# Attention between two routed feed-forward layers: all shared tiles first, batch 1's norm chain later in the ring, stores, loads and bias adds moved

## The chip, the cores and the metric

One core of one Trainium2 chip runs the whole program in one launch. The metric is device time in microseconds (us), the median of several executions. The engines are TensorE (PE, with its weight loads as PEld), VectorE (DVE), ScalarE (ACT), GpSimd (POOL) and SyncE (SP), each with its own program in order; they meet at semaphores. SP, ACT and POOL also issue DMA transfers.

## The reference

The input is `(2, 1024, 128)` float32: two batches of 1024 tokens.

```python
x = x + 0.5 * ffn(layernorm(x))
x = x + attention(layernorm(x))          # 16 heads of 8, causal
x = x + 0.5 * ffn(layernorm(x))

def expert(h, g, u, d):                  # 128 -> 352 -> 128
    return einsum('...i,hi->...h', silu(h @ g.T) * (h @ u.T), d)
def ffn(x):                              # 1 shared expert, top 2 of 7 routed ones
    out = expert(x, sg, su, sd)
    for e in range(7):
        out = out + w[..., e:e+1] * expert(x, rg[e], ru[e], rd[e])
def attention(x):
    v = x @ w_v + v_b
    q = (x @ w_q + q_b) @ w_k.T + k_b    # the keys are x itself
    probs = softmax(causal(q . x / sqrt(8)))
    return (probs @ v) @ c_proj_w + c_proj_b
```

## The kernel before, in words

**First feed-forward layer.** Tokens stand in 16 tiles of 128. The list `JOBS[0]` sets the order of the work: 13 tiles for the shared expert (`BEFORE[0]`), then 38 tiles of routed rows (`NJ`), then the last 3 shared tiles; 54 jobs (`NQ`). At step s PE does the first matmuls of job s (`up_pe`, L899 to L901), the transposes of job s-1 (`act_tr_pe`, L919) and the last matmuls of job s-2 (`down_pe`, L933); ACT does silu (L1000) and a copy (L1008), DVE the product (L1043) and the eviction (L1079 routed, L1081 shared). Routed rows are first sorted by expert: POOL scatters 32 blocks of rows to DRAM (L1174), two halves of 16, and SP loads them back tile by tile (L1260). `batch_at` says ahead of which step PE transposes a batch of loaded tiles (L953); routed tiles 0 to 9 need the first half sorted, tiles 10 and up both. POOL scatters each routed result back to DRAM (L1197), and `results_load` (L1271) reads the results of 8 token tiles, batch 0 after routed tile 21, batch 1 after the last one, 37.

**Between the layers.** The tokens are four chunks of 512 (`NCH`), chunks 0 and 1 being batch 0. For each: weighting (L1126) and adding (L1138) the results, statistics (`n_stats`, L504), `rstd` on POOL (L519), `z` on ACT (L540), transposes (`n_tr`, L573), a high and a low part (`n_hi` L579, `n_lo` L585), queries (`q_pe`, `q_act`, low part L1571 or L1145) and values (`v_pe`, L1508 to L1510, `v_act` L1543, bias L1553). The tables `FRONT_PE`, `BEHIND_ACT` and so on give the step of the feed-forward loop at which batch 0's pieces run; batch 1's pieces on PE and DVE run in the ring, at the places of `SECOND_PE` and `SECOND_DVE`. Keys and queries are written to DRAM (L1578) and read back, one group of 4 heads at a time (L1928, L1936).

**Attention.** 8 groups of 4 heads, 4 to a batch. The row maxima of a group are found first: PE makes the scores (L1605, with a causal mask by L1608), DVE reduces them (L1757). These are "ring" items, at most 4 in flight. The prologue `RING_PROLOGUE` has 54: 38 maxima of group 0, the first of group 1, two transposes of the maxima (`mrow`, L1628), 13 more of group 1. DVE turns the maxima into a high and a low part (L1761 to L1765), copies them out (L1771), and SP writes them into the queries' spare rows (L1949); then the exponent units start: PE L1648, ACT L1816, and PE's products with the values L1677. From then on each group is a body in which PE goes through an order written out by hand (`ORDERS`): units of its group, the last 24 maxima of the next group and the first 14 of the group after that, four of these ahead of that body's `mrow` transposes.

**The queue of SP** in `attn_sp` is a list in order too, and each wait in it holds back all that stands behind. Keys of group 2 share memory with `q_f`, `q_h`, `q_l`, so `keys_clear` (L1421) waits until all queries are stored; the loads of group 2 wait until the clearing has landed.

## Time and profile before

| what | value |
|---|---|
| median of 3 runs | 570.33 us (570.11 to 571.1) |
| profiled execution, its own time | 571.84 us |
| span of its trace | 570.0 us |
| mean granted clock of PE | 0.972 |
| PE busy | 521.1 us, 91% |
| DVE, ACT, POOL busy | 388.5, 319.8, 272.1 us |

Busy shares are means over stages with different limits: first the layer with its sorting (to about 163 us), then the crossing into attention (to about 200 us), attention in bodies of 29.5 us, and the second layer. What a change in one stage is worth has to be read in that stage.

### The profile page before, as it was taken

The page shows a single profiled execution, that of the slowest core. Times are in us where ns is not written, and L with a number is a line of the kernel's source. Part 1 is how long each engine was busy: PE and PEld are TensorE (multiplying, and loading weights), DVE is VectorE, ACT ScalarE, POOL GpSimd, SP SyncE. Part 2 cuts the span into 40 slices and gives each one's busy share as a digit, 9 for nine tenths or more (in the row PEclk, how much of TensorE's full clock was granted, in tenths as well). Part 3 has the DMA queues.
Part 4 walks back from the last instruction along what each step waited for, and adds up shares of the span by engine and source line. Part 5 has one row for each costly group of instructions (what it writes and reads, how often), then busy time and mean ns, then how long its engine had stood idle before and what let it go on. Part 6 is the DMA issues. An engine that isn't in the chain of part 4 may idle for free.

```text
span 570.0 us, 11374 instructions
## 1 busy us (share of the span) xinstructions
PE 521.1 (91%) x3574; PEld 406.0 (71%) x3574; DVE 388.5 (68%) x1013; ACT 319.8 (56%) x678; POOL 272.1 (48%) x417
## 2 busy tenths in 40 slices
PE   5985969999996799999999999999999889889995
PEld 2884969998954465656666666565746889889995
DVE  5694635557367888887979888888555775445744
ACT  4552424457444276776767677677776444434643
POOL 8299887667356711212120303030318888854540
PEclk9899789999996899999999999999999999999999
DMA  8922424132861581505050505020001031431414
GB/s 283 294 67 50 111 77 120 45 107 81 242 183 56 170 190 35 173 2 175 2 174 1 176 0 176 1 102 2 2 2 33 31 91 43 118 92 34 125 50 121
DMA packets 41384, 54.65 MB, mean 96 GB/s; under 512 B 6064, under 2 KB 32176, under 8 KB 40560
## 3 DMA queue, kind: packets, MB, share of 16 engines
q1 hardware_dynamic: 32528, 42.70, 26.4%
q0 software_dynamic: 4480, 9.25, 4.9%
q10 hardware_dynamic: 4320, 1.98, 1.3%
q8 instruction: 32, 0.52, 0.4%
q14 instruction: 24, 0.20, 0.1%
HBM read 34.03 MB, written 28.00 MB: 109 GB/s over the span
## 4 chain that ended last, share of the span: by engine, by line
PE 57%; issue 18%; POOL 10%; DMA 6%; DVE 4%; SPq 2%; ACT 2%; ACTq 1%; another core or an unknown queue 1%; POOLq 0%; DVEq 0%
PE psum L1605 11%; PE psum L1648 11%; PE psum L1677 10%; PE psum L933 6%; POOL z_rows L1174 6%; PE psum L919 3%; PE psum L901 3%; PE psum L899 3%; PE psum L900 3%; PE psum L1608 2%; POOL idle L1184 2%; DMA b_p<-in_attn_c_proj_b 2%; DMA yc<-y_rows 1%; DMA y_rows<-ys,to_row 1%; PE psum L1633 1%
## 5 line engine op out<-in xcount | busy, mean ns | idle before, releaser
L1757 DVE TENSOR_REDUCE mxp<-psum 128x1 f32<-128x512 f32 (+3 forms) x304 | 179.0, 654 | 32.9 <-PE psum L1605 32.1
L1816 ACT ACTIVATE probs<-psum 128x512 f32<-128x512 f32 (+1 forms) x304 | 154.9, 578 | 39.8 <-PE psum L1648 37.2
L1863 POOL TENSOR_SCALAR_AFFINE_SELECT probs<-probs 128x512 f32<-128x512 f32 x64 | 40.0, 635 | 174.2 <-ACT probs L1816 174.2
L1648 PE MATMUL psum<-queries,keys 128*128 128x512 f32 (+3 forms) x384 | 122.5, 381 | 0.6 <-DMA queries<-m_rows 0.3
L1605 PE MATMUL psum<-keys,queries 128*128 128x512 f32 (+1 forms) x304 | 116.1, 417 | 2.9 <-DVE mxp L1757 2.4
L1000 ACT ACTIVATE silu<-psum 128x352 f32<-128x352 f32 x107 | 49.6, 463 | 99.5 <-PE psum L901 62.6
L1197 POOL DMA_INDIRECT y_rows<-ys,to_row x76 | 74.3, 977 | 59.1 <-DVE ys L1079 35.4
L1043 DVE TENSOR_TENSOR act<-silu,psum 128x352 f32<-128x352 f32 x107 | 55.6, 519 | 68.0 <-ACT silu L1000 41.7
L933 PE MATMUL psum<-wall_f,at 128*128 (+1 forms) x648 | 92.2, 279 | 2.7 <-DVE x L1081 1.8
L1648 PEld LDWEIGHTS psum<-queries,keys 128*128 128x128 f32 x384 | 66.8, 191 | 26.8 <-ACT probs L1816 12.6
L933 PEld LDWEIGHTS psum<-wall_f,at 128*128 128x128 f32 x648 | 82.1, 194 | 4.1 <-ACT at L1008 2.3
L1605 PEld LDWEIGHTS psum<-keys,queries 128*128 128x128 f32 x304 | 58.1, 194 | 18.1 <-DVE mxp L1757 7.8
L1677 PE MATMUL psum<-probs,vg 128*32 128x512 f32 (+3 forms) x768 | 69.8, 491 | 0.4 <-POOL probs L1863 0.4
L919 PE MATMUL psum<-ident,act 128*128 128x128 f32 x324 | 54.7, 278 | 5.9 <-DVE act L1043 4.4
L899 PE MATMUL psum<-wall,zs_h 128*128 x152 | 56.9, 374 | 1.0 <-issue 1.0
L1008 ACT COPY at<-psum 128x384 f32<-128x384 f32 x108 | 51.3, 475 | 11.0 <-PE psum L919 9.7
L900 PE MATMUL psum<-wall,zs_h 128*128 x152 | 50.4, 331 | 0.0
L901 PE MATMUL psum<-wall,zs_l 128*128 x152 | 50.2, 330 | 0.0
L919 PEld LDWEIGHTS psum<-ident,act 128*128 128x128 f32 x324 | 41.0, 142 | 12.3 <-DVE act L1043 8.2
L1677 PEld LDWEIGHTS psum<-probs,vg 128*32 128x32 f32 x768 | 21.1, 109 | 35.4 <-issue 22.9
L1174 POOL DMA_INDIRECT z_rows<-zrow,slots x32 | 34.4, 1076 | 15.9 <-DVE slots L750 10.5
L1174 POOL DMA_INDIRECT z_rows<-zrow_late,slots x32 | 31.2, 975 | 5.8 <-issue 5.8
(240 smaller groups left out, 732.4 us busy)
## 6 DMA issues: line engine op xcount, KB each, us to landing
z_rows<-q_stack SPq DMA_DIRECT2D x12, 682.5 KB, 5.6
keys<-k_stack SPq DMA_DIRECT2D x32, 128.0 KB, 5.9
queries<-q_stack SPq DMA_DIRECT2D x8, 512.0 KB, 5.3
zg_early<-z_rows SPq DMA_DIRECT2D x44, 65.0 KB
yc<-y_rows SPq DMA_DIRECT2D x10, 256.0 KB, 4.0
zg_late<-z_rows SPq DMA_DIRECT2D x32, 65.0 KB
k_stack<-zt_h SPq DMA_DIRECT2D x8, 256.0 KB, 2.9
q_stack<-q_h SPq DMA_DIRECT2D x8, 256.0 KB, 3.7
```

Source lines behind the costliest of these rows:

```text
L899: e.matmul(dst, zh, weight(K.wall, base, hi, HID), start=True, stop=False)
L900: e.matmul(dst, zh, weight(K.wall, base, lo, HID), start=False, stop=False)
L901: ins = e.matmul(dst, zl, weight(K.wall, base, hi, HID), start=False, stop=True)
L919: ins = e.transpose(bank(K, at_bank(f, q))[:, k * P:(k + 1) * P], K.act[:, q % 2, k * P:(k + 1) * P], K.ident[:, :])
L933: ins = e.matmul(bank(K, Y_BANK)[:, 0:EMB], K.at[:, q % 2, k * P:(k + 1) * P], weight(K.wall_f, base, DN + k * EMB, EMB), start=(k == 0), ...
L1174: e.indirect_dma_start(K.z_dram[f], bass.IndirectOffsetOnAxis(ap=K.slots[:, g:g + 1], axis=0), K.zrow[f][:, t, :], None).then_inc(K.z_sc[t ...
L1197: e.indirect_dma_start(K.y_dram[f], bass.IndirectOffsetOnAxis(ap=K.to_row[:, j:j + 1], axis=0), K.ys[:, j % RING_Y, :], None).then_inc(K.y ...
L1605: ins = e.matmul(dst, K.queries[u][:, i * P:(i + 1) * P], K.keys[u][:, heads[0]:heads[-1] + 1, k0 * P:(k0 + nb) * P], start=True, stop=Tru ...
L1648: ins = e.matmul(slot(K, u, d, n)[:, m * (q1 - q0):(m + 1) * (q1 - q0)], K.keys[v][:, j, kt * P:(kt + 1) * P], K.queries[v][:, q0:q1], sta ...
L1677: ins = e.matmul(bank(K, O_BANK)[32 * j:32 * j + 32, q0 - half * CHUNK:q1 - half * CHUNK], K.vg[:, kt, j, :], probs_of(K, n)[:, j, :], sta ...
L1757: e.tensor_reduce(K.mxp[:, heads[0]:heads[-1] + 1, i, which], scores, AX.X, ALU.max).then_inc(K.A["taken"], 1)
L1816: e.activation(probs_of(K, product)[:, heads[0]:heads[-1] + 1, :], src, ACT.Exp, scale=SCALE).then_inc(K.A["ex"], 1)
```

## The change

Six edits, each an order of work:

1. `BEFORE[0]` is 16: all shared tiles stand ahead of the routed ones, and the batch with routed tile 10 is transposed one step later relative to the tiles.
2. The values of batch 0 (`v` 0 and 1) leave the loop's last steps and run in the ring, ahead of items 0 and 2; ACT evicts them behind the issue of batch 1's `results_load`. They use banks 6 and 4.
3. Batch 1's pieces stand 5 or 6 items later in the ring.
4. On SP, chunk 1's queries are stored for heads 0 to 3 first, group 0's queries are loaded on that, and the other 12 heads are stored behind.
5. The store of batch 1's keys moves from SP to ACT; the store of its queries moves on SP from ahead of `rows_load` (L1949) to behind it.
6. `proj_bias_pool` (L2060), four adds in a row on POOL at the crossing, becomes two ahead of `v_bias_pool(0)` and two inside attention, behind the bodies of groups 1 and 2.

```diff
-BEFORE = (13, 11)
+BEFORE = (TT, 11)
-ONE_AT_AGAIN = (43, NQ)
+ONE_AT_AGAIN = (46, NQ)
 def batch_at(f, step):
-        if step == BEFORE[f] + j - (min(b, 2) if f == 0 else 1 if j == WHOLE else 2):
+        if step == BEFORE[f] + j - min(2 if f else b, 1 if j == WHOLE else 2):
...
 def v_pe(K, c):
     if c == 0:
-        e.wait_ge(K.A["qf"], 1)
+        e.wait_ge(K.A["qf"], 2)
     elif c == 1:
-        e.wait_ge(K.A["qf"], 2)
+        e.wait_ge(K.FF[0]["yev"], NQ)
...
-SECOND_DVE = {13: (("n_stats", 2),), 16: (("n_stats", 3),), 20: (("n_lo", 2),), 26: (("n_lo", 3),)}
+SECOND_DVE = {18: (("n_stats", 2),), 21: (("n_stats", 3),), 26: (("n_lo", 2),), 32: (("n_lo", 3),)}
...
         elif r == 2:
-            e.wait_ge(K.A["vev"], 1)
+            e.wait_ge(K.A["qf"], 1)
...
 def attn_pool(K):
     e = K.nc.gpsimd
+    e.wait_ge(K.NS[1]["z"], NCH)
     e.wait_ge(K.A["vb"], NCH)
     for p in range(LOOP3):
         for u in range(3):
             pool_body(K, p, u, LOOP)
+            if (p, u) in ((0, 1), (0, 2)):
+                proj_bias_pool(K, u + 1)
...
 def attn_sp(K):
-    for c in range(NCH // 2):
-        keys_sp(K, c)
-        queries_sp(K, c)
+    keys_store(K, e, 0)
+    queries_sp(K, 0)
+    keys_store(K, e, 1)
+    queries_sp(K, 1, (0, 4))
     for c in range(NCH // 2):
         e.wait_ge(K.k_st[c], 16 * 3)
     e.wait_ge(K.wiped, 2 * WIPES)
     keys_load(K, 0, 0, 0)
-    for c in range(NCH // 2):
-        e.wait_ge(K.q_st[c], 16 * 3)
+    e.wait_ge(K.q_st[0], 16 * 3)
+    e.wait_ge(K.q_first, 16 * 3)
+    queries_load(K, 0, 0, 0)
+    queries_sp(K, 1, (4, HEADS))
     e.wait_ge(K.FF[0]["mix"], 4)
-    queries_load(K, 0, 0, 0)
     keys_load(K, 0, 0, 1)
+    e.wait_ge(K.q_st[1], 16 * 3)
     queries_load(K, 0, 0, 1)
-    for c in range(NCH // 2, NCH):
-        keys_sp(K, c)
+    rows_load(K, 0, 0, 0, RING_PROLOGUE.index(("mrow", 0, 0)))
     for c in range(NCH // 2, NCH):
         queries_sp(K, c)
-    rows_load(K, 0, 0, 0, RING_PROLOGUE.index(("mrow", 0, 0)))
     for c in range(NCH // 2, NCH):
         e.wait_ge(K.k_st[c], 16 * 3)
         e.wait_ge(K.q_st[c], 16 * 3)
     keys_clear(K, 2)
...
             results_load(K, e, 0, 1, (0, 1))
+            v_act(K, 0)
+            v_act(K, 1)
...
             q_act(K, 2)
+            keys_store(K, e, 2)
             q_act(K, 3)
+            keys_store(K, e, 3)
```

On PE, where the first layer ends and the ring begins, before (`wall_f,at` are the last matmuls of a job, `keys,queries` ring items 0 and 1, `ident_b,mask_b` their masks):

```order
L900 MATMUL psum<-wall,zt_h 128x352
L901 MATMUL psum<-wall,zt_l 128x352
L919 MATMUL psum<-ident,act 128x128 x3
L933 MATMUL psum<-wall_f,at 128x128 x3
L919 MATMUL psum<-ident,act 128x128 x3
L933 MATMUL psum<-wall_f,at 128x128 x6
L1605 MATMUL psum<-keys,queries 128x512
L1608 MATMUL psum<-ident_b,mask_b 128x512
```

The same place in the changed kernel (`wv,zt` are the value matmuls, 12 to a chunk; the last three of chunk 0, ring items 0 and 1, and the first three of chunk 1):

```order
L1509 MATMUL psum<-wv_h,zt_h 128x128
L1510 MATMUL psum<-wv_l,zt_h 128x128
L1511 MATMUL psum<-wv_h,zt_l 128x128
L1607 MATMUL psum<-keys,queries 128x512
L1610 MATMUL psum<-ident_b,mask_b 128x512
L1607 MATMUL psum<-keys,queries 128x512
L1610 MATMUL psum<-ident_b,mask_b 128x512
L1509 MATMUL psum<-wv_h,zt_h 128x128
L1510 MATMUL psum<-wv_l,zt_h 128x128
L1511 MATMUL psum<-wv_h,zt_l 128x128
```

The shared tile ahead of the ring is gone, and the value matmuls of batch 0 now stand around its first two items.

On SP, at the crossing, before (`queries<-m_rows` is `rows_load`, `keys<-q_stack` is `keys_clear`, the last two rows are the loads of group 2):

```order
L1578 DMA q_stack<-q_h 16x8x512 x2
L1578 DMA q_stack<-q_l 16x8x512
L1578 DMA q_stack<-q_h 16x8x512 x2
L1578 DMA q_stack<-q_l 16x8x512
L1949 DMA queries<-m_rows 4x8x128 x2
L1421 DMA keys<-q_stack 32x4096 x4
L1928 DMA queries<-q_stack 128x1024
L1936 DMA keys<-k_stack 32x1024 x4
```

On SP, the same place in the changed kernel, from the load of group 0's queries on:

```order
L1934 DMA queries<-q_stack 128x1024
L1579 DMA q_stack<-q_h 12x8x512 x2
L1579 DMA q_stack<-q_l 12x8x512
L1942 DMA keys<-k_stack 32x1024 x4
L1934 DMA queries<-q_stack 128x1024
L1955 DMA queries<-m_rows 4x8x128 x2
L1579 DMA q_stack<-q_h 16x8x512 x2
L1579 DMA q_stack<-q_l 16x8x512
L1579 DMA q_stack<-q_h 16x8x512 x2
L1579 DMA q_stack<-q_l 16x8x512
L1422 DMA keys<-q_stack 32x4096 x4
```

The six stores of batch 1's queries have moved from ahead of the maxima's transfer to between it and the clearing; the load of group 0's queries stands ahead of 12 heads' stores.

## Rows read from the trace of the kernel before

**Rows 1.** Windows: length, busy PE, PEld, DVE, ACT, POOL, granted clock, DMA share, GB/s.

```profile
163.70:193.60 29.90, 22.57 (x84) 13.73 (x83) 25.67 (x56) 14.22 (x33) 17.22 (x26) 0.83 0.42 126
196.40:199.80 3.40, 3.13 (x8) 1.50 (x8) 2.87 (x6) 0.00 (x0) 1.44 (x2) 0.53 0.34 77
205.00:234.50 29.50, 29.50 (x204) 18.68 (x203) 24.33 (x48) 20.65 (x41) 5.52 (x10) 1.00 0.49 130
```

**Rows 2.** PE in order of time: start, duration; in brackets idle before, releaser.

```profile
56.44 0.50 PE L953 MATMUL psum<-ident,zg_early 128*128 128x128 f32 x2 [4.90 <-DMA zg_early<-z_rows]
82.05 0.66 PE L953 MATMUL psum<-ident,zg_early 128*128 128x128 f32 x2 [4.67 <-DMA zg_early<-z_rows]
149.51 0.31 PE L1508 MATMUL psum<-wv_h,zt_h 128*128 128x128 f32 x1
150.88 0.38 PE L899 MATMUL psum<-wall,zs_h 128*128 x1
162.84 0.48 PE L1605 MATMUL psum<-keys,queries 128*128 128x512 f32 x1
```

**Rows 3.** The chain that ended last: start, duration, what.

```profile
76.18 2.39 DMA z_rows<-zrow,slots
96.69 0.67 PE psum L933 x6
98.67 0.67 PE psum L933 x6
...
158.96 4.07 DMA y_rows<-ys,to_row
163.70 3.52 DMA yc<-y_rows
```

**Rows 4.** DVE from the last routed tile to the maxima's parts.

```profile
158.39 0.29 DVE L1079 COPY ys<-psum 128x128 f32<-128x128 f32 x1
163.12 0.29 DVE L1081 SCALAR_TENSOR_TENSOR x<-psum,x 128x128 f32<-128x128 f32 x1 [1.09 <-PE psum L933]
163.70 7.33 DVE L1757 TENSOR_REDUCE mxp<-psum 128x4 f32<-128x512 f32 x13
179.41 0.69 DVE L1757 TENSOR_REDUCE mxp<-psum 128x1 f32<-128x512 f32 x1 [1.93 <-PE psum L1605]
193.90 1.19 DVE L1763 CAST mm_hl<-nmax 128x32 fp32r<-128x32 f32 x1
195.13 1.20 DVE L1765 TENSOR_TENSOR mm_hl<-nmax,mm_hl 128x32 fp32r<-128x32 f32 x1
223.06 0.52 DVE L1763 CAST mm_hl<-nmax 128x32 fp32r<-128x32 f32 x1
```

**Rows 5.** POOL beside the maxima's parts.

```profile
192.57 4.93 POOL L2060 TENSOR_TENSOR x<-x,b_p 128x512 f32<-128x512 f32 x4
```

**Rows 6.** SP's queue in order of time.

```profile
148.79 1.16 SPq L1578 DMA_DIRECT2D q_stack<-q_h  x2
197.15 1.27 SPq L1949 DMA_DIRECT2D queries<-m_rows  x2
210.65 0.34 SPq L1928 DMA_DIRECT2D queries<-q_stack  x1
211.03 1.82 SPq L1936 DMA_DIRECT2D keys<-k_stack  x4
```

**Rows 7.** DMA issues: count, KB each, median us to landing; first row whole run.

```profile
queries<-q_stack SPq DMA_DIRECT2D x8, 512.0 KB, 5.3
...
q_stack<-q_l SPq DMA_DIRECT2D x2, 256.0 KB, 3.6
...
keys<-k_stack SPq DMA_DIRECT2D x2, 128.0 KB, 5.2
```

**Rows 8.** PE: the first exponent unit, and the first maximum of group 2.

```profile
199.86 0.53 PE L1648 MATMUL psum<-queries,keys 128*128 128x512 f32 x1 [0.26 <-DMA queries<-m_rows]
221.86 0.40 PE L1605 MATMUL psum<-keys,queries 128*128 128x512 f32 x1
```

More of the change, by code:

```diff
@@ L465, in place_memory @@
     K.q_st = [sem(f"q_st{c}") for c in range(NCH)]
+    K.q_first = sem("q_first")
     K.k_st = [sem(f"k_st{c}") for c in range(NCH)]
@@ L1572, in q_dve, with stack_store, keys_store, queries_sp @@
      .then_inc(K.A["ql"], 1)
[L1575 to L1582 removed]
+def stack_store(e, dram, part, c, src, s, heads=(0, HEADS)):
+    (b, half), (h0, h1) = divmod(c, 2), heads
+    dst = dram[b * HEADS + h0:b * HEADS + h1, 8 + 8 * part:16 + 8 * part, half * CHUNK:(half + 1) * CHUNK]
+    e.dma_start(dst, src[h0 * HDIM:h1 * HDIM, :].bitcast(F32)).then_inc(s, 16)
+def keys_store(K, e, c):
+    cols = slice(c * CHUNK, (c + 1) * CHUNK)
     e.wait_ge(K.NS[1]["lo"], c + 1)
[L1584 to L1589 removed]
+    stack_store(e, K.k_dram, 0, c, K.zt_h[1][:, cols], K.k_st[c])
+    stack_store(e, K.k_dram, 1, c, K.zt_l[1][:, cols], K.k_st[c])
+    stack_store(e, K.k_dram, 2, c, K.zt_h[1][:, cols], K.k_st[c])
+def queries_sp(K, c, heads=(0, HEADS)):
     e, u = K.nc.sync, c % 2
+    done = K.q_first if heads == (0, 4) else K.q_st[c]
     e.wait_ge(K.A["ql"], c + 1)
[L1592 to L1594 removed]
+    stack_store(e, K.q_dram, 0, c, K.q_h[:, u, :], done, heads)
+    stack_store(e, K.q_dram, 1, c, K.q_h[:, u, :], done, heads)
+    stack_store(e, K.q_dram, 2, c, K.q_l[:, u, :], done, heads)
 def m_unit_pe(K, n, r_bank, u):
@@ L2051, in proj_x_dve, with proj_bias_pool @@
     e.tensor_tensor(xc, xc, bank(K, PM_BANK[c]).rearrange("p (t e) -> p t e", e=EMB), ALU.add).then_inc(K.A["xup"], 1)
-def proj_bias_pool(K):
-    e = K.nc.gpsimd
-    e.wait_ge(K.NS[1]["z"], NCH)
-    for c in range(NCH):
-        xc = K.x[:, c * TPC:(c + 1) * TPC, :]
-        e.tensor_tensor(xc, xc, K.b_p[:, :].unsqueeze(1).to_broadcast([P, TPC, EMB]), ALU.add).then_inc(K.A["bp"], 1)
+def proj_bias_pool(K, c):
+    xc = K.x[:, c * TPC:(c + 1) * TPC, :]
+    K.nc.gpsimd.tensor_tensor(xc, xc, K.b_p[:, :].unsqueeze(1).to_broadcast([P, TPC, EMB]), ALU.add)\
+     .then_inc(K.A["bp"], 1)
 EARLY_PE = [(), (("proj_tr", 0), ("proj_tr", 1), ("proj", 0), ("proj", 1)),
@@ L2085 @@
              15: (("lists", (1, 0)),), 16: (("lists", (1, 1)),), 17: (("lists", (1, 2)),), 18: (("lists", (1, 3)),)}
-BEHIND_DVE = [{0: (("query", 0),), **{2 * k + 3: (("weights_lo", m),) for k, m in enumerate(ROUTED_WEIGHTS)}, 19: (("small", 0),), 22: (("weights", 0),), 39: (("mix", 0),), 40: (("n_stats", 0),), 41: (("mix", 1),), 42: (("n_stats", 1),), 43: (("n_lo", 0),),
-              45: (("q_lo", 0),), 46: (("n_lo", 1),), 48: (("q_lo", 1),)},
+BEHIND_DVE = [{0: (("query", 0),), **{2 * k + 3: (("weights_lo", m),) for k, m in enumerate(ROUTED_WEIGHTS)}, 19: (("small", 0),), 22: (("weights", 0),), 42: (("mix", 0),), 43: (("n_stats", 0),), 44: (("mix", 1),), 45: (("n_stats", 1),),
+               46: (("n_lo", 0),), 48: (("q_lo", 0),), 49: (("n_lo", 1),), 51: (("q_lo", 1),)},
               {0: (("proj_lo", 2), ("proj_lo", 3)), 1: (("x", 2), ("stats", 2), ("x", 3), ("stats", 3)), 2: (("z", 3),),
@@ L2282, in _ @@
             scatters_pool(K, 0)
+            e.wait_ge(K.NS[1]["z"], 2)
+            proj_bias_pool(K, 0)
+            proj_bias_pool(K, 1)
             v_bias_pool(K, 0)
@@ L2293, in _ @@
             v_bias_pool(K, 3)
-            proj_bias_pool(K)
             attn_pool(K)
```

35 lines of the change are left out of this document (11 added, 24 removed).

## The prediction

> **What bounds the kernel now.** I read the busy shares first, then the windows, PE in order of time, DVE in order of time, and last the chain that ended last and SP's queue. PE is busy 91% of the span, but in attention it is busy in all of a body of 29.5 us [rows 1]: what delays a body's start delays the end by the same, and PE idle inside a body is never given back. So the change is worth what it moves the first exponent unit, which starts at 199.86 [rows 8], less whatever it makes PE wait behind it. Ahead of that unit PE has two idle stretches, before 56.44 and before 82.05, 4.90 and 4.67 us, both waiting for loaded rows [rows 2]. The second ends with POOL's sorting: its last scatter starts at 76.18 and lands 2.39 us later [rows 3], and no edit touches that. From 163.70 to 193.6, group 0's maxima, DVE is busy 25.67 of 29.90 us [rows 1]: DVE sets the pace and stands idle for 4.2.
>
> **Shared tiles first.** A job costs PE 1.98 us (98.67 less 96.69) [rows 3]. Three shared jobs, 5.9 us, start where PE now falls idle (56.44 - 4.90 = 51.5 [rows 2]) and end near 57.4, 1 us behind the arrival of the first rows. That small delay is paid from the second idle stretch, as is routed tile 8, which now runs ahead of the wait for tile 10's rows. At 82.05 PE has done 3 + 1 = 4 more jobs. Batch 0's results need the routed tiles up to 21, one job less behind 82.05: its queries and keys come 2.0 us earlier. The eviction of the last routed tile stood at 158.39 [rows 4]. It comes earlier by one job (2.0), by two value products no longer ahead of it (150.88 - 149.51 = 1.37 each [rows 2], 2.7), and because no job follows it: the last two steps take 1.09 + 0.29 = 1.38 [rows 4] in place of 1.98 (1.2). Sum 5.9, so 152.5. The scatters, the load and the weighting of batch 1 follow, 5.9 earlier. The whole layer, last eviction 163.12 [rows 4], ends 10.6 earlier.
>
> **What is late next: group 0's queries.** The ring can't use all 10.6. SP issued chunk 1's query store at 148.79 [rows 6], now at 146.8. The last of the three small stores starts some 1.2 later and lands in at most 3.6 [rows 7], at 151.6; the keys' four issues (1.8 [rows 6]) fit ahead of that. Then the queries: 512 KB, 5.3 us by the run's median [rows 7], so 157.0, where ring item 0 stood at 162.84 [rows 2]: 5.8 earlier, and DVE's first maximum at 157.9.
>
> **The ring.** Its work stays 25.7 us [rows 1]. Of the 4.2 idle, the longest piece, 1.93 before 179.41 [rows 4], is item 19 waiting behind chunk 2's transposes, 15.7 us behind the start of the results' load at 163.70 [rows 3]. That load now starts at 157.8 (5.9 earlier, behind a scatter's landing of 4.07 [rows 3]), so the item behind the transposes could run at 173.5; it is item 25 now, which DVE reaches only near 174 (157.9, 25 items at 0.6, one statistics piece). This wait and small ones around it go. New idle: the second value product stands between items 1 and 2 (1.37 of PE against DVE's work on two items, about 0.9 lost); `n_tr` and queries at item 30 and queries and values at 35 to 38 (about 0.6 each, my estimate from PE pieces of 1.4 us against three items in flight). So 2.1 idle: the maxima end at 157.9 + 25.7 + 2.1 = 185.7, against 193.6: 7.9 earlier. The statistics at items 18 and 21 cost nothing while the results land before 163; at 157.8 + 3.5 [rows 3] they land at 161.3.
>
> **The bias adds.** DVE's cast and subtraction of the maxima take 1.19 and 1.20 us while POOL's four adds run (192.57 to 197.50), and the same cast takes 0.52 in the next body, beside masks [rows 4, 5]. With the adds gone I take 0.5 and 0.2: 1.7 us, of which 0.5 goes again, since item 38 comes behind the values of chunk 3. Net 1.2. Beside the cast POOL may now run `v_bias_pool(2)`, adds of a quarter of the size (128x128 against 128x512, 4.93 us for four [rows 5]): should each of the two DVE instructions wait for one, the gain is some 0.6 less. The Trainium skill (SBUF — State Buffer, Who interferes with whom) says that a cast and an operation with two inputs in SBUF can need the port pair that VectorE shares with GpSimd, and that whoever comes first holds it for a whole instruction. By that rule the two waits shrink with the length of POOL's adds and don't vanish, the sum would be some 0.6 worse than with none, and maxima that are reduced from PSUM wait for nobody; the trace agrees with the first part, its numbers being the two rows above. The two adds inside attention lie in POOL's idle (5.5 of 29.5 busy [rows 1]); the two ahead of `v_bias_pool(0)` fill time in which POOL waited for values. If they did delay the weighting, they would cost 2.5 at most, less some 2 of slack.
>
> The first unit so starts at 199.86 - 7.9 - 1.2 = 190.8: 9.1 earlier.
>
> **What the SP order gives back.** Six stores now stand between the maxima's transfer and the clearing. Before, the clearing was issued right behind that transfer (197.15 + 1.27 [rows 6]), 1.4 us ahead of the first unit; group 2's loads followed at 210.65, 12.1 later, the last of them started by 212.5 and took 5.2 [rows 6, 7]: there at 217.7, 17.8 behind the first unit. Group 2's first maximum, the fourth ring item ahead of that body's transposes, ran at 221.86 [rows 8], 22.0 behind the first unit, with 4.2 to spare. The stores take six issues at about 0.6 (1.16 for two [rows 6]), and the last one's landing 3.6 [rows 7]: 3.0 + 3.6 = 6.6 to 7.2. So the data is there 24.4 to 25.0 behind the first unit, and PE, whose order is fixed, waits 2.4 to 3.0; I take 2.7. Queued behind that item are group 0's units and products, so ACT and DVE wait too. The keys' stores on ACT (6 issues, 3.6 us) are hidden by its idle time (busy 14.2 of 29.9 in the ring [rows 1]), whose last copy of values then ends near 187, ahead of the first unit by more than its table load. The new banks of `v` 0 and 1 cost nothing: both are free when the layer ends.
>
> **Sum.** 571.84 - 9.1 + 2.7 = 565.4 for a profiled execution; the runs' median is 1.5 below the profiled time (570.33), so 563.9.
>
> **The rivals.**
> - *No wait at group 2.* The clearing could land faster or the six issues go out at once. The ring would keep all 9.1: 561.2. Against it: the clearing moves 2 MB, and its 12.1 us passed with nothing beside it. 0.17.
> - *The wait and the clock.* After an idle stretch ahead of 196.4 the granted clock read 0.53 (the lower level, 1.2 GHz) for 3.4 us [rows 1]. If the new wait does the same inside a body, where PE is the bound, half of 3.4 us is lost: 1.7. With the wait as taken 565.6; with a wait of 3.5 and a ring start 0.8 later as well, 567.2. 0.20.
> - *The layer's end doesn't carry over.* The load of group 0 meets the stores, both groups' loads and the scatters within 10 us and lands 3 us late, so the ring gains 3 less: 566.9. 0.05.
> - *Slower.* One mechanism, the same load: to cost more than all, group 0's queries must land 5.3 + 6.4 = 11.7 us behind their issue, at 163.4. Every microsecond beyond adds one; at 13 us the time is 571.6. Against it, the run's median of 5.3 over eight such loads. 0.05.
>
> The forecast itself has 0.53, with its own range 562.2 to 565.9 (a wait of 1.5 to 4, a ring start within 0.8).
>
> **How the numbers follow.** A measurement of this kernel tells about 0.2%, 1.1 us, from no change. All cases but the last gain more, save a part of the third; the slower case straddles it. Faster 0.91, within 0.2% 0.04, slower 0.05. The range leaves out the slower case and the ends of the others: 560.8 to 567.8.
>
> **What the profile would show.** PE without idle before 56 and with some 4 to 5 us before 82; the last eviction of the layer near 152.5; ring item 0 near 157; the cast at 0.5 or less; the first unit near 190.8; and PE idle 2 to 3 us on the first maximum of group 2, released by a DMA into `keys`, near 213. The prediction is wrong if that wait is missing, if item 0 starts behind 159, or if the ring has idle time that I don't see.

## The result

| | median | runs | ratio to before (95%) |
|---|---|---|---|
| before, beside the changed kernel | 572.53 us | 20 | |
| changed kernel | 568.22 us (564.23 to 570.52) | 20 | 0.9927 (0.9907 to 0.9948) |

The change is faster by 0.73%, 4.2 us. The forecast was 6.4 us less than 570.33, and 568.22 is above its range, 560.8 to 567.8. Of the 4.3 us between 563.9 and 568.22, 2.2 are the level of the kernel before, which stood at 572.53 in these runs and not at 570.33. The other 2.1 are the forecast's own. With the level taken out, 570.33 times the ratio is 566.2: inside the whole range, but above the 562.2 to 565.9 of the forecast's own case. So about half of the miss in the number is the level of the reference, and the other half is a mechanism that came out otherwise. One execution of the kernel before, in a later round, took 978.39 us and is left out of the ratios.

**The profile after.** The profiled execution took 568.2 us, where the forecast's sum for one was 565.4; its span is 565.9 (570.0 before), the mean granted clock 0.976 (0.972). It is one execution, and so is each trace below. First PE in order of time, the pieces of the prediction's steps and the last transpose of the maxima (brackets: idle before, releaser):

```profile
58.31 0.38 PE L954 MATMUL psum<-ident,zg_early 128*128 128x128 f32 x2
82.00 0.66 PE L954 MATMUL psum<-ident,zg_early 128*128 128x128 f32 x2 [2.79 <-DMA zg_early<-z_rows]
...
156.73 0.71 PE L1607 MATMUL psum<-keys,queries 128*128 128x512 f32 x1 [2.47 <-DMA queries<-q_stack]
175.29 1.09 PE L574 MATMUL psum<-ident,z 128*128 128x128 f32 x4 [1.50 <-issue]
191.41 0.47 PE L1650 MATMUL psum<-queries,keys 128*128 128x512 f32 x1 [1.58 <-DMA queries<-m_rows]
217.08 0.47 PE L1607 MATMUL psum<-keys,queries 128*128 128x512 f32 x1 [3.62 <-DMA keys<-k_stack]
222.02 0.27 PE L1630 MATMUL psum<-ident,mm_hl 128*32 128x128 f32 x1
```

Against [rows 2, 8]: the stretch before 56.44 is gone, ring item 0 came at 156.73 (forecast 157.0) where it stood at 162.84, the first unit at 191.41 (190.8) where it stood at 199.86. Then PE waits 3.62 us for group 2's keys, in which the kernel before had no wait. DVE, from the last routed tile's eviction to the maxima's parts, against [rows 4]:

```profile
153.00 0.29 DVE L1080 COPY ys<-psum 128x128 f32<-128x128 f32 x1 [1.21 <-issue]
161.15 9.13 DVE L1760 TENSOR_REDUCE mxp<-psum 128x4 f32<-128x512 f32 x16 [1.65 <-PE psum L1607]
186.95 0.25 DVE L1764 TENSOR_REDUCE nmax<-mxp 128x32 f32<-128x96 f32 x1
187.24 0.18 DVE L1766 CAST mm_hl<-nmax 128x32 fp32r<-128x32 f32 x1
187.46 0.19 DVE L1768 TENSOR_TENSOR mm_hl<-nmax,mm_hl 128x32 fp32r<-128x32 f32 x1
```

SP's queue behind the maxima, against [rows 6]:

```profile
188.77 1.18 SPq L1955 DMA_DIRECT2D queries<-m_rows  x2
190.00 1.22 SPq L1579 DMA_DIRECT2D q_stack<-q_h  x2
191.59 0.54 SPq L1579 DMA_DIRECT2D q_stack<-q_l  x1
192.19 1.24 SPq L1579 DMA_DIRECT2D q_stack<-q_h  x2
193.47 0.60 SPq L1579 DMA_DIRECT2D q_stack<-q_l  x1
197.00 1.73 SPq L1422 DMA_DIRECT2D keys<-q_stack  x4
209.97 0.34 SPq L1934 DMA_DIRECT2D queries<-q_stack  x1
```

Windows (length, busy PE, PEld, DVE, ACT, POOL, granted clock, DMA share, GB/s):

```profile
190.00:192.00 2.00, 0.59 (x3) 0.55 (x4) 1.57 (x3) 0.75 (x2) 1.25 (x4) 1.00 0.41 93
...
217.08:222.02 4.94, 4.94 (x21) 3.88 (x21) 2.94 (x5) 2.69 (x6) 0.63 (x1) 0.65 0.00 0
230.00:259.50 29.50, 29.50 (x202) 18.55 (x201) 24.66 (x48) 20.54 (x41) 6.66 (x10) 1.00 0.23 73
```

The bodies are as they were: 29.50 us, all PE. So the books are closed by one milestone, the second transpose of the maxima in group 0's body, the last row of PE above. In the kernel before this transpose, which I call the milestone, stands here:

```profile
225.22 0.27 PE L1628 MATMUL psum<-ident,mm_hl 128*32 128x128 f32 x1
```

From the first unit to it took 25.36 us before (225.22 - 199.86) and 30.61 now (222.02 - 191.41). Of the 5.25 more, 3.62 are the wait; 1.58 come behind it: group 2's first maximum to the milestone took 3.36 (225.22 - 221.86) and takes 4.94 with the clock at 0.65 in the mean (the window from 217.08), for most of it at the lower level, 1.2 GHz. So 8.45 us gained at the first unit, 5.25 given back: 3.2 are left, 3.4 at the last body (SP issues its maxima at 397.37, before at 400.79), 4.1 in the span and 3.6 in the time of the two executions (571.84 and 568.2).

### The profile page after: what moved, and what is told of

The parts are those of the page before. It is cut to its first block, busy times and chain, and to the rows that moved or that the text cites. A ratio compares the mean times of both kernels' runs of the same rounds, so it can differ in the third digit from the quotient of the medians.

```text
span 565.9 us, 11380 instructions
## 1 busy us (share of the span) xinstructions
PE 520.9 (92%) x3574; PEld 405.6 (72%) x3574; DVE 387.3 (68%) x1013; ACT 319.7 (56%) x678; POOL 272.2 (48%) x417
## 4 chain that ended last, share of the span: by engine, by line
PE 61%; issue 12%; DVE 11%; DMA 9%; SPq 4%; ACT 1%; ACTq 1%; POOL 0%; DVEq 0%; POOLq 0%
PE psum L1650 11%; PE psum L1607 10%; PE psum L1679 10%; PE psum L934 7%; PE psum L920 4%; PE psum L900 3%; PE psum L901 3%; PE psum L902 3%; DVE mxp L1760 2%; PE psum L1610 2%; DMA b_p<-in_attn_c_proj_b 2%; DMA keys<-q_stack 2%; DMA k_stack<-zt_h 1%; PE psum L1635 1%; PE psum L954 1%
## 5 line engine op out<-in xcount | busy, mean ns | idle before, releaser
L1009 ACT COPY at<-psum 128x384 f32<-128x384 f32 x108 | 51.3, 475 | 12.1 <-PE psum L920 8.6
L900 PE MATMUL psum<-wall,zs_h 128*128 x152 | 56.0, 368 | 1.7 <-DVE zs_l L1068 1.7
L901 PE MATMUL psum<-wall,zs_h 128*128 x152 | 49.7, 327 | 0.0
```

What stands on the lines that cost most here:

```text
L900: e.matmul(dst, zh, weight(K.wall, base, hi, HID), start=True, stop=False)
L901: e.matmul(dst, zh, weight(K.wall, base, lo, HID), start=False, stop=False)
```

## The experiments

Twelve kernels, each timed beside the kernel before, four to a chip. The changed kernel was not timed in these rounds; its row has the runs of the result, so two of these kernels are compared through their ratios to the kernel before. All but the one named so start from the changed kernel. Executions of one kernel lie up to 5 us from their median, so a difference of two ratios below about 0.3% says nothing; the traces are read at their marks (times in us).

| kernel | item 0 | maxima done | first unit | wait at group 2 | milestone | maxima done to milestone | ratio (95%) |
|---|---|---|---|---|---|---|---|
| before | 162.84 | 193.62 | 199.86 | none | 225.22 | 31.60 | 1 |
| changed | 156.73 | 186.95 | 191.41 | 3.62 | 222.02 | 35.07 | 0.9927 (0.9907 to 0.9948) |
| all stores first | 157.63 | 188.34 | 196.30 | none | 222.96 | 34.62 | 0.995 (0.9925 to 0.9975) |
| both values first | 156.99 | 186.99 | 191.45 | 2.51 | 219.39 | 32.40 | 0.9921 (0.9896 to 0.9946) |
| matmuls in the wait | 155.92 | 186.95 | 191.41 | filled | 219.80 | 32.85 | 0.9922 (0.9895 to 0.995) |
| four adds back | 156.59 | 187.61 | 192.06 | 2.93 | 222.00 | 34.39 | 0.9932 (0.9906 to 0.9958) |
| queries in one piece | 160.03 | 190.54 | 195.09 | 2.54 | 224.63 | 34.09 | 0.9957 (0.9923 to 0.9991) |
| shared tiles as before | 161.70 | 189.86 | 194.33 | 2.77 | 222.55 | 32.69 | 0.9943 (0.9917 to 0.997) |
| stores spread | 157.75 | 189.71 | 196.33 | none | 224.31 | 34.60 | 0.9925 (0.9894 to 0.9956) |
| spread, both values | 157.16 | 187.72 | 194.24 | none | 220.92 | 33.20 | 0.9936 (0.9903 to 0.9969) |
| chunk 2's stores ahead | 157.98 | 188.69 | 193.79 | none | 219.28 | 30.59 | 0.9897 (0.9862 to 0.9933) |
| the same, both values | 158.36 | 188.75 | 193.97 | none | 219.55 | 30.80 | 0.9896 (0.9858 to 0.9933) |
| before, stores behind | 163.06 | 193.93 | 200.53 | 2.44 | 228.45 | 34.52 | 1.0054 (1.0025 to 1.0084) |
| both values, matmuls | 155.87 | 186.06 | 190.56 | filled | 217.95 | 31.89 | 0.9899 (0.9867 to 0.9932) |

"Maxima done" is the start of DVE's last step on them (`nmax`); the column behind the milestone is what an edit to SP's queue has to be judged by, since item 0 alone differs by more than 1 us between executions that have nothing different ahead of it. It is noisy itself. In five kernels nothing differs in the order of SP's queue from the maxima's transfer on: changed, both values first, four adds back, queries in one piece, shared tiles as before. Their waits at group 2 are 3.62, 2.51, 2.93, 2.54 and 2.77 us, the mean 2.9, and the column reads 32.40 to 35.07. The changed kernel's trace has the longest wait of the five.

Behind the wait there are two cases and nothing between them. From group 2's first maximum to the milestone it takes 4.94 us in the changed kernel, with four adds back (222.00 - 217.06) and with queries in one piece (224.63 - 219.69), where the granted clock fell to 0.50. It takes 3.38 or 3.39 with both values first, with the shared tiles as before and in the kernel before with stores behind, where it stayed at 1.00, and 3.36 in the kernel before. So the lower clock costs 1.6 us each time, and it fell in three of the five.

### All stores first

```diff
-    rows_load(K, 0, 0, 0, RING_PROLOGUE.index(("mrow", 0, 0)))
     for c in range(NCH // 2, NCH):
         queries_sp(K, c)
+    rows_load(K, 0, 0, 0, RING_PROLOGUE.index(("mrow", 0, 0)))
```

> The changed kernel with one edit: on SP the stores of batch 1's queries stand ahead of rows_load again, as in the kernel before; all else stays changed. Theory A: what the change gave back is the order of SP's queue: PE's wait of 3.62 us on the first maximum of group 2 (and 1.6 us at the lower clock behind it) comes from six stores between the maxima's transfer and the clearing. Then the clearing starts some 5 us earlier, PE's wait on group 2 is gone and the time falls by 4.5 to 5.3 us below the changed kernel. Rival B: the clearing itself (12 to 13 us for 2 MB) is what is late and the stores only stand in its shadow: then the wait shrinks by less than 1 us. Rival C: the stores ahead of the maxima's transfer delay it (the last of them can only be issued near 188.8, where the transfer was issued at 188.77), so the first unit comes later by about what the wait loses, and the time stays within 1 us of the changed kernel.

SP and then PE:

```profile
189.58 1.57 SPq L1579 DMA_DIRECT2D q_stack<-q_h  x2
192.65 1.54 SPq L1955 DMA_DIRECT2D queries<-m_rows  x2
```

```profile
196.30 0.77 PE L1650 MATMUL psum<-queries,keys 128*128 128x512 f32 x1 [4.54 <-DMA queries<-m_rows]
```

The wait at group 2 is gone and stands ahead of the first unit instead, 4.9 us later than in the changed kernel. The maxima's transfer is issued behind chunk 3's stores, and lands in 2.1 us behind its last issue, where it took 1.46 (191.41 - 189.95). The lower clock goes with the wait: 0.50 from 196 to 198. This is rival C; the wait is moved, not removed.

### Both value products first

```diff
-SECOND_PE = {0: (("v", 0),), 2: (("v", 1),), 25: ...
+SECOND_PE = {0: (("v", 0), ("v", 1)), 25: ...
```

> The changed kernel with the value product of chunk 1 ahead of ring item 0 (in PE's idle time before group 0's queries land) and not between items 1 and 2. Theory A: DVE's idle of 1.65 us behind item 1 is lost for good, because DVE sets the ring's pace: the first unit comes 1.5 to 1.9 us earlier and the time falls by as much. PE also stays at work ahead of item 0, so its clock may not fall there. Rival: the ring is held further on by batch 1's results (the norm's transposes wait on POOL's adds and statistics), which stay where they are: then the first unit moves by less than 0.5 us.

```profile
175.27 1.09 PE L574 MATMUL psum<-ident,z 128*128 128x128 f32 x4 [2.37 <-issue]
191.45 0.47 PE L1650 MATMUL psum<-queries,keys 128*128 128x512 f32 x1 [1.59 <-DMA queries<-m_rows]
```

```profile
176.82 0.69 DVE L1760 TENSOR_REDUCE mxp<-psum 128x1 f32<-128x512 f32 x1 [1.31 <-PE psum L1607]
```

The rival is right. DVE's idle stretch behind item 1 is gone, but chunk 2's transposes run at 175.27, where they ran at 175.29 in the changed kernel. PE's idle time ahead of them has grown from 1.50 to 2.37, DVE now waits 1.31 us for the item behind them, and the first unit has not moved. So here batch 1's results set the ring, not its first items: POOL has added them at 171.5, in the changed kernel at 171.1. In the changed kernel DVE has no gap at that place; there the two limits come to the same time. The milestone is 2.6 us earlier all the same, at an equal first unit: the wait is 2.51 and the clock stays up behind it. No edit stands behind the first unit that could explain it; it is the difference between executions that the table shows, and the ratio, 0.9921, has none of it.

### Matmuls in the wait

```diff
             if n == 0:
+                if (p, u, d) == (0, 0, 2):
+                    for _ in range(7):
+                        busy_pe(K, bank(K, r_bank))
                 e.wait_ge(K.ld_k[v], 80 * loads(p, u, d))
```

> The changed kernel with 14 dummy matmuls (128x512, bf16) on PE behind the ring bank's release and ahead of the wait for group 2's keys; they write into the bank that the item overwrites. They take some 3.2 us, inside the wait of 3.6. Theory A: the wait costs more than its length, because the granted clock is at the lower level behind it: from the first maximum of group 2 to the next body took 8.29 us, 6.71 in the kernel before. With PE at work the wait stays 3.6 us in all and the 1.6 us behind it come back: 1.2 to 1.7 us below the changed kernel. Rival: what stands behind the wait is slow for another reason (ACT or DVE refilling, DMA traffic), and the time stays the same within 0.5 us.

```profile
213.38 3.20 PE L1718 MATMUL psum<-ident_b,ones_b 128*128 128x512 bf16 x14
216.39 0.50 PE L1607 MATMUL psum<-keys,queries 128*128 128x512 f32 x1
...
219.80 0.27 PE L1633 MATMUL psum<-ident,mm_hl 128*32 128x128 f32 x1
```

With the same first unit (191.41) the milestone comes 2.2 us earlier, and the granted clock from 217 to 220 is 1.00. Two things are in the 2.2. Group 2's first maximum runs at 216.39, 0.7 us before the changed kernel's, which is within what the wait varies by. From there to the milestone it takes 3.41 in place of 4.94: 1.5 us are the clock's. In the timed runs this doesn't show (0.9922 against 0.9927).

### The four bias adds back in a row

The adds go back into one piece at the start of `attn_pool`.

> The changed kernel with the four bias adds back on POOL in a row ahead of attention, as before. Theory A: DVE's cast and subtraction of the maxima again wait for POOL's adds, 1.2 us each in place of 0.18 and 0.19: the first unit comes 1.7 to 2.1 us later and the time rises by as much, the wait at group 2 unchanged because the clearing moves along. Rival: the adds would now not meet the cast, because POOL reaches them at another time relative to DVE (values are evicted by ACT behind two key stores): then the change is below 0.5 us.

```profile
187.89 0.18 DVE L1766 CAST mm_hl<-nmax 128x32 fp32r<-128x32 f32 x1
```

```profile
188.13 3.37 POOL L1552 TENSOR_TENSOR v_all<-v_all,b_v 128x128 f32<-128x128 f32 x8 [0.57 <-ACT v_all L1542]
191.46 5.00 POOL L2064 TENSOR_TENSOR x<-x,b_p 128x512 f32<-128x512 f32 x4
```

The rival is right, and the cast stays at 0.18: the adds now start 3.9 us behind the maxima's end, where they started 1.0 ahead of it (192.57 against 193.62). POOL comes to them only behind the values of chunks 2 and 3, which edit 3 had put 6 items later. The milestone stands at 222.00 (222.02) and the ratio is 0.9932: no run here shows edit 6 to be worth anything.

### Queries of group 0 in one piece

Edit 4 undone: `queries_sp(K, 1)` for all heads, both stores and the layer's last sum waited for ahead of the loads.

> Undoes one part of the change: chunk 1's queries are stored in one piece for all eight heads, both groups' loads follow both stores and the layer's last sum (FF[0]['mix'] at 4), as in the kernel before; all else is the changed kernel. My theory A (behind the layer, the ring's start hangs on group 0's queries, and loading them ahead of the rest is worth something): SP's next issues wait for the sum, which stands behind the layer's last addition near 155 to 156, and for a store of three pieces twice as large, so group 0's queries are issued some 1.5 to 3 us later and land near 159; ring item 0 near 158.5 to 160 in place of 156.7. The whole delay reaches the end only if the ring isn't held elsewhere: ring items behind chunk 2's transposes hang on batch 1's results (PE waited 1.50 us for these at 175.29 in the changed kernel), so of a delay of 2 to 3 us about 1 to 1.5 is swallowed there and the first unit comes at 192 to 193 (changed kernel: 191.41). Rival B (the load isn't what holds item 0, the layer's end is): item 0 at 156.7 to 157.2, first unit at 191.4. Behind the first unit the wait at group 2 stays the same 3 to 4 us by both, for the stores stand where they stood. Ratio to the kernel before: A 0.994 to 0.998; B 0.993.

```profile
160.03 0.79 PE L1605 MATMUL psum<-keys,queries 128*128 128x512 f32 x1 [3.72 <-DMA queries<-q_stack]
```

Item 0 is 3.3 us late, as theory A had it; the first unit is 3.7 later than in the changed kernel, more than the 1 to 2 expected, and 2.6 are left at the milestone.

This run shows a price of edit 4 as well. The load of batch 1's results is issued at 162.18 here and ACT starts to weight them 4.0 us later, at 166.21, as in the kernel before. In the changed kernel it takes 5.7:

```profile
163.28 2.06 ACTq L1271 DMA_DIRECT2D yc<-y_rows  x4
167.31 4.79 ACT L1126 ACTIVATE yc<-yc,w 128x128 f32<-128x128 f32 x16 [5.81 <-DMA yc<-y_rows]
```

```profile
158.64 2.15 ACTq L1272 DMA_DIRECT2D yc<-y_rows  x4
164.36 4.79 ACT L1127 ACTIVATE yc<-yc,w 128x128 f32<-128x128 f32 x16 [2.45 <-DMA yc<-y_rows]
```

The first pair is the kernel before, the second the changed kernel. Edit 4 lets SP issue group 1's queries, 512 KB, within 1.2 us of that load (at 159.30 in the changed kernel); in the kernel before and here they go out some 6 us ahead of it. In all eleven kernels with the edit it takes 4.7 to 6.2 us, in the three without it 4.0 to 4.1.

### Shared tiles as before

Edit 1 undone: `BEFORE[0] = 13`, the steps of batch 0's chain back at their slots.

> Undoes only the order of the jobs: thirteen shared tiles, the routed tiles, then the last three shared tiles, with the steps of batch 0's chain back at the slots that they had before; the value products stay in the ring, the stores stay where the change put them. Theory A (the layer's end is worth its whole delay once it is later than the load): PE falls idle before 56.4 for some 4.9 us again and before 82 for 4.7, the last routed tile comes about 3.2 us later (of the 5.9 forecast, 2.0 for the job and 1.2 for the steps go; the values' 2.7 stay) and the layer's last eviction near 159.5 to 160.5; ring item 1 needs the layer's end, so DVE's first maximum goes to 160.5 or later (157.92 in the changed kernel), the first unit to 193.5 to 194.5 (191.41); the wait at group 2 is unchanged at 3 to 4 us. Ratio to the kernel before 0.998 to 1.001. Rival B (the order of the jobs is worth nothing at the end, the ring's start comes from the values and the split load alone): first unit at 191.4 to 192, ratio 0.993.

```profile
81.94 0.66 PE L954 MATMUL psum<-ident,zg_early 128*128 128x128 f32 x2 [4.45 <-DMA zg_early<-z_rows]
...
161.70 0.45 PE L1607 MATMUL psum<-keys,queries 128*128 128x512 f32 x1
...
219.16 0.47 PE L1607 MATMUL psum<-keys,queries 128*128 128x512 f32 x1 [2.77 <-DMA keys<-k_stack]
```

Ring item 0, now held by PE (no idle time ahead of it), comes 5.0 us later, the first unit 2.9, the milestone only 0.5. The ring takes less time: PE comes to it without a pause, the granted clock stays at 1.00, and the second value product costs DVE 0.74 us of idle time where it cost 1.65 and 0.19. Between the last two marks the wait is 0.85 shorter and no lower clock stands behind it, which is the difference between executions again. The ratio, 0.9943, is below theory A's 0.998 to 1.001; it can't be told from the changed kernel's. So edit 1 is shown to move the ring's start, and not shown to shorten the time.

### Stores spread, with and without the second value product

```diff
+    queries_sp(K, 2)
     rows_load(K, 0, 0, 0, RING_PROLOGUE.index(("mrow", 0, 0)))
-    for c in range(NCH // 2, NCH):
-        queries_sp(K, c)
...
             v_act(K, 3)
+            queries_sp(K, 3, e=e)
             attn_act(K)
```

> Takes the suspected cause away without changing the amount of work: chunk 2's query stores go out on SP ahead of the maxima's transfer (they are ready at 184, when SP is idle), chunk 3's go out on ACT behind its last copy of values, so no store stands between the maxima's transfer and the clearing. Theory A (edit 5's stores on SP, and nothing else, make PE wait at group 2's first maximum, and the lower granted clock behind it is its consequence): the clearing is issued near 192 (197.05 in the changed kernel), ends near 204.5, group 2's keys land by 212 and PE doesn't wait there (wait 0 to 0.3 us, before group 2's first maximum near 213.5); the clock stays at 1.0 to the next body, which starts at 220.2 to 221 (225.37). If the first unit stays at 191.4 to 192.4 the time falls by 3.5 to 5 us against the changed kernel: ratio to the kernel before 0.983 to 0.988. Rival B (the wait comes from the amount of traffic at that time, or the clearing runs slower next to units and products): the loads still land at 214 or later, wait 1 us or more. Rival C (the stores beside the maxima's transfer hold it as they did with all stores ahead of it): the first unit moves to 193 to 196, and the gain is 0 to 3 us; ratio 0.988 to 0.993.

> As the kernel with spread stores, and the second value product stands ahead of ring item 0 too, as in the kernel with both products first. Theory A: the time of the kernel with spread stores within 0.2%, for the ring is held at chunk 2's transposes by batch 1's results, whatever PE does ahead of them; first unit at 191.4 to 192.4, ratio to the kernel before 0.983 to 0.988. Rival: DVE's earlier start gives 0.5 to 1 us at the first unit, ratio 0.981 to 0.986, and a difference to the kernel with spread stores that the intervals may not tell apart. It is run as the best version candidate.

PE's first unit in the first of them and in the second, then the windows of the second:

```profile
196.33 0.77 PE L1650 MATMUL psum<-queries,keys 128*128 128x512 f32 x1 [3.77 <-DMA queries<-m_rows]
```

```profile
194.24 0.47 PE L1650 MATMUL psum<-queries,keys 128*128 128x512 f32 x1 [3.64 <-DMA queries<-m_rows]
```

```profile
188.00:190.00 2.00, 2.00 (x10) 0.97 (x10) 1.67 (x6) 1.07 (x2) 0.47 (x2) 1.00 1.02 341
190.00:192.00 2.00, 0.60 (x3) 0.18 (x2) 2.00 (x4) 0.00 (x0) 2.00 (x6) 1.00 0.95 328
194.50:197.50 3.00, 3.00 (x11) 2.43 (x11) 2.26 (x4) 2.28 (x4) 0.00 (x0) 0.67 0.78 180
```

Both are rival C, the first with its unit at 196.33 just above that rival's 193 to 196; the second misses both of its own ranges, with the first unit at 194.24 and a ratio of 0.9936. There is no PE wait at group 2, but the first unit comes 6.6 and 6.5 us behind the maxima (4.46 in the changed kernel). In the two windows from 188 to 192 341 and 328 GB/s are moved, where the changed kernel's second one has 93: the DMA engines are full, and the maxima, two transfers of 16 KB, stand among three stores of 256 KB. PE's wait is now there, and the lower clock follows it there (0.67).

### Chunk 2's stores ahead, with and without the second value product

```diff
+    queries_sp(K, 2)
     rows_load(K, 0, 0, 0, RING_PROLOGUE.index(("mrow", 0, 0)))
-    for c in range(NCH // 2, NCH):
-        queries_sp(K, c)
+    queries_sp(K, 3)
```

> The changed kernel with chunk 2's query stores ahead of the maxima's transfer on SP; chunk 3's stay behind it. The runs so far leave two accounts of edit 5: (A) the stores' data, 768 KB a chunk at some 330 GB/s, is what a transfer behind them waits for, so the question is only whether the queues are empty when the maxima's transfer comes (near 188.8); (B) any store ahead of the transfer holds it. By A chunk 3's keys and chunk 2's queries (1.5 MB from about 184, 4.6 us) are through by 189, the first unit stays at 191.4 to 192, the clearing goes out 1.8 us earlier relative to the maxima's transfer (three issues) and the wait at group 2 falls from 3.6 to 1 to 2 us; ratio to the kernel before 0.987 to 0.992. By B the first unit slips by 2 us or more, as in the kernels with all stores ahead and with spread stores, the wait at group 2 vanishes and the time is no better: 0.992 to 0.995.

> The same, and the second value product ahead of ring item 0. Run as a candidate for the best version. A: first unit as in the kernel with chunk 2's stores ahead, wait at group 2 of 0.5 to 2 us, ratio to the kernel before 0.986 to 0.992, not to be told from that kernel's. B: first unit 2 us later, no wait, 0.992 to 0.995.

SP, PE and windows of the first:

```profile
190.51 1.56 SPq L1955 DMA_DIRECT2D queries<-m_rows  x2
196.49 1.73 SPq L1422 DMA_DIRECT2D keys<-q_stack  x4
```

```profile
193.79 0.47 PE L1650 MATMUL psum<-queries,keys 128*128 128x512 f32 x1 [2.23 <-DMA queries<-m_rows]
...
219.28 0.27 PE L1630 MATMUL psum<-ident,mm_hl 128*32 128x128 f32 x1
```

```profile
190.00:192.00 2.00, 1.55 (x6) 0.67 (x5) 1.94 (x5) 0.99 (x2) 1.42 (x4) 1.00 1.04 365
```

In what happens behind the maxima this is theory A, and better than it said; in the first unit it isn't, for 193.79 is 2.4 later than in the changed kernel where A had 191.4 to 192. Of that, 1.7 are a ring that ended later (188.69). The clearing is issued 7.8 us behind the maxima's end (10.05 in the changed kernel); no wait at group 2 is left, where 1 to 2 us were expected, and no lower clock. The first unit comes 0.6 later behind the maxima's end (5.10 against 4.46), for the queues are full to 192. From the maxima's end to the milestone it takes 30.59, 4.5 less than in the changed kernel, 1.8 less than in the best of the five kernels with all stores behind (32.40) and 1.0 less than before the change. The second value product changes nothing (30.80).

### Before, with the stores behind

The same move of `rows_load` ahead of `queries_sp` as in edit 5, and nothing else, in the kernel before.

> The kernel BEFORE with one edit: chunks 2 and 3's query stores behind the maxima's transfer on SP. It does edit 5 alone. In the kernel before all stores are issued by 192.8 and the queues are empty (0 GB/s) from 196, ahead of the transfer at 197.15, so there is nothing for edit 5 to gain there. Theory A (six issues of 0.6 and a landing of about 3 move the clearing by 6 to 7 us, against 4.2 us to spare at group 2): first unit unchanged within 0.5 us (199.9), PE waits 2 to 3.6 us at group 2's first maximum, released by a DMA into keys, and up to 1.6 more goes at the lower clock where it falls; ratio 1.003 to 1.009. Rival B (the wait at group 2 in the changed kernel comes from something else that the change does, such as the ring's pace or the other engines): no wait, ratio 1.000 within 0.002.

```profile
225.07 0.47 PE L1605 MATMUL psum<-keys,queries 128*128 128x512 f32 x1 [2.44 <-DMA keys<-k_stack]
...
228.45 0.27 PE L1628 MATMUL psum<-ident,mm_hl 128*32 128x128 f32 x1
```

This half of edit 5 makes the wait by itself: 2.44 us where there was none, the milestone 3.2 us later, the time 0.54% longer. Rival B is out. Here the wait left the clock at 1.00: of the 2.9 us more between the maxima's end and the milestone, 2.44 are the wait and 0.4 stand ahead of the first unit.

### Both values first, matmuls in the wait

Both edits from above, with ten matmuls.

> The changed kernel with two of the edits tried: the second value product ahead of item 0, and ten idle matmuls (their result is overwritten) in PE's wait at group 2. Theory A: first unit 191.4 to 191.8, the loads for group 2 land when they landed (216), the ten matmuls take some 2.2 of the 2.5 us of wait and leave the clock at 1.00 behind it; next body as in the kernel with both products first, 222.5 to 223.5; ratio to the kernel before 0.990 to 0.993. Rival: the wait left in is shorter than the matmuls and they cost 0.3 to 0.8 us; ratio 0.992 to 0.995.

```profile
212.46 2.33 PE L1718 MATMUL psum<-ident_b,ones_b 128*128 128x512 bf16 x10
214.44 0.58 PE L1607 MATMUL psum<-keys,queries 128*128 128x512 f32 x1
```

The earliest milestone, 217.95, partly for a ring that started 0.9 us earlier than in the changed kernel. The matmuls run right up to group 2's first maximum, so the trace doesn't tell whether they or the keys ended the wait. 0.9899, like the two kernels with chunk 2's stores ahead. These three lie below the changed kernel's 0.9927 by 0.3%, and their intervals overlap with its own: each is a better candidate than the changed kernel, none is shown to be faster.

## Why the forecast was right in direction and too large

**Shared tiles first: right.** The stretch before 56.44 is gone, and the last routed eviction stands at 153.00 (152.5). The stretch before 82 shrank from 4.67 to 2.79. The forecast named 4 to 5, against its own working, by which 1 us and routed tile 8's 2.0 are paid from it. With edit 1 undone item 0 comes 5.0 us later.

**Group 0's queries as the new bound: right,** to 0.3 us (156.73 against 157.0; executions differ by more than that, so some of it is luck). With them in one piece item 0 moves to 160.03, released by the same load.

**The ring: right in its steps, 1.2 us short.** Maxima were done at 186.95 against 185.7. DVE stood idle for 3.2 us (0.19, 1.65, 0.74 and 0.63) where I had 2.1. The second value product cost 1.8 of it where I had 0.9, since it ran at the lower clock, 2.5 us (158.20 to 160.66) in place of 1.37. The other two came to 1.4 for the 1.2 that I had estimated. Taking the product away gives nothing, though: with both products first the maxima still end at 186.99. The results behind chunk 2's transposes bind at the same time, and I had them too early, an item ready at 173.5, where the transposes alone run at 175.29 (177.85 before). The last scatter was 5.4 us earlier, as forecast within 0.5, but ACT issued the results' load only 4.6 earlier, and it weights them only 2.95 earlier (164.36 for 167.31), since edit 4 had put group 1's queries beside that load. POOL's bias on the values, now ahead of its adds, isn't what held them: POOL waits 0.93 us for ACT behind it.

**The bias adds: right in effect, wrong in cause.** The cast and subtraction fell to 0.18 and 0.19 (0.5 and 0.2 taken), but not through edit 6: with the adds back in a row they are 0.18 and 0.19 too, since the values of chunks 2 and 3, moved by edit 3, hold POOL until the maxima are through. In both kernels where POOL's adds of 128x512 began ahead of the cast it took 1.19 (before, and before with stores behind). That agrees with what the Trainium skill (SBUF — State Buffer, Who interferes with whom) says of the shared port pair. The small wait that I had allowed for on `v_bias_pool(2)` didn't come in the changed kernel, by luck: its bias starts at 187.47, 0.01 us behind the start of the subtraction, which takes 0.19.

**The first unit** so came at 191.41, 0.6 later than forecast: 1.2 late at the maxima, 0.6 of it back from the cast and subtraction.

**What the SP order gives back: the step that failed.** It is the sentence "PE ... waits 2.4 to 3.0; I take 2.7" with nothing behind the wait. The traced execution gave back 5.2 us in its place: 3.62 of wait and 1.58 of lower clock. That is 2.5 us more than taken, where the whole execution came 2.8 above its 565.4; the first unit adds 0.6, and 0.3 came back behind the ring.

*The wait: right in kind, and 0.9 too small in this execution.* Of its parts, the six issues and their landing were right: the clearing was issued 5.6 us behind the first unit (197.00 - 191.41), where it had been 1.3 ahead of it (198.59 - 199.86), so 6.9 later against 6.6 to 7.2. The clearing itself, taken at its old 12.1 us, took 13.0 (197.00 to 209.97). 6.9 and 0.9, less 4.2 to spare, are 3.6. It took 12.4 to 13.0 in the eight kernels with both chunks' stores behind the maxima and 12.0 to 12.4 in the other six; why wasn't found. Over the five kernels with this order the wait is 2.9 in the mean, so 2.7 was a fair size, and this trace drew a long one.

*The lower clock behind the wait: left at zero, cost 1.58.* It was the rival "the wait and the clock", priced at 1.7 with a chance of 0.20; its worse case, a wait of 3.5 and a ring start 0.8 late, is nearly what the trace shows, and its 567.2 lies about 1 us from both 568.22 and 566.2. In three of five kernels with this order the clock fell behind the wait, and each time the stretch to the milestone took 4.94 us for 3.4. With matmuls in the wait the clock stayed at 1.00 and the stretch took 3.41. That stretch lasted 3.0 us (213.38 to 216.39) and a bare wait of 2.77 us left the clock up, so the matmuls alone don't prove what would have come without them; the price, 1.6 us wherever the clock fell, is shown. The mistake was to leave it at nothing, when by these traces it came more often than not.

**The sum again.** -8.45 at the first unit, +3.62 and +1.58 behind it: -3.2 at the milestone, and 4.1 in the span, 4.2 by the ratio. The 0.9 to 1.0 between lies behind the ring. The stretch from the last body's maxima to the end differs by up to 3.8 us among these kernels (166.8 to 170.6), none of which touches it, so the 0.7 us that it is shorter in the changed kernel's trace can't be put down to the change.

**Of the rivals,** "no wait at group 2" and "slower" are refuted by the trace. "The layer's end doesn't carry over" is too: the last routed tile was 5.4 us earlier (158.39 to 153.00), item 0 6.1.

## What to carry to other kernels

A queue in fixed order is a budget: six stores put ahead of a long transfer cost what they take, less the slack that the transfer's reader had. Neither "all ahead" nor "all behind" was best here; by the traces it was the stores whose data is there ahead of the urgent transfer, and the rest behind it. The timed runs point the same way and don't settle it. A wait that a change creates inside a stage bound by PE costs its length and can cost a stretch at half clock behind it, as the 3.62 us here did; price both. A single trace can draw a long or a short wait from the same order of work, here 2.51 to 3.62, so a size is read from several. When several edits act on one place, an effect that appears may belong to another edit than the one meant for it, and only undoing one at a time tells.

## What the runs showed of the hardware

- **PE's idle time and its clock.** Inside attention, at the first unit or at group 2, the granted clock fell to the lower level behind single waits of 2.93 (four adds back), 3.62, 3.64, 3.77 and 4.54 us, and stayed at 1.00 behind 2.23, 2.36, 2.44, 2.51 and 2.77 us. Behind 2.54 us (queries in one piece) it fell, 0.50 from 221 to 224. At the ring's start it fell behind much shorter waits: in the changed kernel behind 2.47 us (0.50 from 158 to 160), with both values first behind 1.02 us (0.50 from 158 to 160); it stayed at 1.00 behind 0.58 (spread, both values) and 0.73 us (both values, matmuls). So the length of the wait alone doesn't tell the cases apart; what does isn't settled here. With matmuls of no use in the wait at group 2 the clock stayed up, in both kernels that have them.
- **Small transfers behind large ones.** The first unit, which waits for the maxima (two transfers of 16 KB), came 4.5 us behind the maxima's end in the changed kernel and in the six made from it that keep all stores behind, 5.1 and 5.2 with one chunk's stores ahead, 6.5 to 8.0 with both chunks' stores ahead or beside. At 328 to 365 GB/s the engines were full (share 0.95 to 1.04).
- **Two loads at once.** The results' load, 1 MB, took 4.0 to 4.1 us from its issue to its reader in the three kernels where group 1's queries had gone out some 6 us ahead of it, and 4.7 to 6.2 in the eleven where they went out within 1.2 us of it.
- **A short cast ends with POOL's instruction.** In the kernel with all stores first POOL, then DVE:

```profile
188.28 1.27 POOL L1146 TENSOR_TENSOR q_l<-q_f,q_h 128x512 fp32r<-128x512 f32 x1 [3.17 <-ACT q_h L1566]
```

```profile
188.63 0.96 DVE L1766 CAST mm_hl<-nmax 128x32 fp32r<-128x32 f32 x1
```

The cast of 128x32 takes 0.96 and ends at 189.59, POOL's subtraction at 189.55; with POOL idle at its start it takes 0.18. With the shared tiles as before it is 0.46, ending at 190.61 beside a subtraction that ends at 190.57. In the kernel before, the cast ends at 195.09 and POOL's second add at 195.03 (four adds of 1.23 from 192.57), and the subtraction behind it ends the same way beside the third. So the wait is what is left of the one POOL instruction that is running, and not a share of its bandwidth. The rule that the Trainium skill gives (SBUF — State Buffer, Who interferes with whom) says the same, and these numbers agree with it.
